# Transformer block and a conditioned norm on one core: row statistics one unit later, and four units of sixteen reduce before they gate

## What is computed

```
def _ada_rmsnorm(x, t, gamma_w, beta_w):
    return (t @ gamma_w.T)[:, None, :] * _rmsnorm(x) + (t @ beta_w.T)[:, None, :]
# attention: 16 heads of 16, softmax(scale * q k^T) v, then W_o
# swiglu: silu(x @ gate_w.T) * (x @ hidden_w.T) @ out_w.T + out_b, 1024 hidden
x = x + a_alpha * _attention(_ada_rmsnorm(x, t, ...), W_q, W_k, W_v, W_o)
x = x + f_alpha * _swiglu(_ada_rmsnorm(x, t, ...), gate_w, hidden_w, out_w, out_b)
# second layer, on the result:
out = (x - mean) * rsqrt(var + EPS) * weight + bias
out = (out + tanh(t @ lin_w.T + lin_b)[:, None, :]) * weight + bias
```

## Time and profile before

| | |
|---|---|
| median of 3 runs | 755.42 us (753.26 to 757.49) |
| profiled execution | 757.3 us, span 755.5 us |
| busy: PE, DVE, ACT, POOL | 94%, 71%, 62%, 52% of the span |
| granted TensorE clock, mean | 0.988 |
| DMA | 107.17 MB, mean 142 GB/s |

### The profile page before, as it was taken

How to read it: one execution, slowest core, us unless ns; L and a number is a source line. 1 busy time by engine, 2 the same in 40 slices (tenths; PEclk the granted TensorE clock), 3 DMA queues, 4 the chain that set the end, 5 groups by cost and what they waited for, 6 DMA issues and landing times.

```text
span 755.5 us, 17410 instructions
## 1 busy us (share of the span) xinstructions
PE 710.5 (94%) x6660; PEld 499.4 (66%) x6660; DVE 533.5 (71%) x797; ACT 466.6 (62%) x860; POOL 391.4 (52%) x493
## 2 busy tenths in 40 slices
PE   5698999999999999999999999999999999999996
PEld 4443435557677667767677677766777667679895
DVE  3877787877577776877677867777677776336765
ACT  4457787776567666775666756675667655753431
POOL 4255142553368534865367543775267444872533
PEclk9879999999999999999999999999999999999998
DMA  8666558355543645263454736255363620332210
GB/s 227 169 211 224 199 175 283 102 183 172 167 135 117 201 148 155 62 217 134 139 163 124 205 107 206 63 179 134 128 178 106 203 81 3 88 96 61 53 48 29
DMA packets 63275, 107.17 MB, mean 142 GB/s; under 512 B 10480, under 2 KB 18344, under 8 KB 63192
## 3 DMA queue, kind: packets, MB, share of 16 engines
q1 hardware_dynamic: 61892, 104.66, 45.1%
q10 hardware_dynamic: 1172, 1.20, 0.6%
q0 software_dynamic: 128, 0.20, 0.1%
HBM read 57.50 MB, written 37.52 MB: 126 GB/s over the span
## 4 chain that ended last, share of the span: by engine, by line
PE 72%; DMA 8%; DVE 8%; ACT 5%; issue 3%; SPq 1%; POOL 1%; ACTq 0%; POOLq 0%; DVEq 0%
PE ps_x L1479 17%; PE ps_o L1455 13%; PE ps_j L1350 11%; PE ps_o L1492 10%; PE ps_s L1439 8%; PE ps_m L1420 6%; DVE mx L1170 3%; ACT prob L963 2%; DMA out_scratch<-o_raw 2%; DMA reciprocal_scratch<-d_s 1%; DMA prob<-in_wk 1%; PE ps_m L1479 1%; PE ps_j L1388 1%; DMA d_c<-reciprocal_scratch 1%; PE ps_s L1479 1%
## 5 line engine op out<-in xcount | busy, mean ns | idle before, releaser
L1170 DVE TENSOR_REDUCE mx<-ps_m 128x2 f32<-128x1024 f32 x211 | 256.9, 1217 | 43.0 <-PE ps_m L1420 42.6
L963 ACT ACTIVATE prob<-ps_s 128x1024 f32<-128x1024 f32 x219 | 223.5, 1020 | 46.6 <-PE ps_s L1439 44.4
L1455 PE MATMUL ps_o<-prob,v 128*32 128x512 f32 x1024 | 128.3, 604 | 0.1
L1439 PE MATMUL ps_s<-qs,ks 64*128 64x512 f32 x438 | 101.2, 456 | 9.6 <-issue 4.4
L670 POOL TENSOR_TENSOR a_lo<-act_y,a_hi 128x256 fp32r<-128x256 f32 x100 | 73.5, 735 | 70.0 <-ACT a_hi L996 70.0
L1211 DVE SCALAR_TENSOR_TENSOR act_y<-act_y,ps_x 128x256 f32<-128x256 f32 x109 | 45.8, 420 | 73.9 <-ACT act_y L989 73.9
L1420 PE MATMUL ps_m<-ks,qs 64*128 64x512 f32 x422 | 90.2, 422 | 8.0 <-DVE mx L1170 4.8
L1479 PE MATMUL ps_x<-n_x,gh_hi 64*128 64x256 f32 x872 | 96.6, 279 | 0.2 <-DMA n_x<-n 0.2
L1479 PE MATMUL ps_x<-n,gh_hi 64*128 64x256 f32 x872 | 96.4, 279 | 0.0
L1439 PEld LDWEIGHTS ps_s<-qs,ks 64*128 64x128 f32 x438 | 41.5, 184 | 77.1 <-issue 52.0
L1479 PEld LDWEIGHTS ps_x<-n,gh_hi 64*128 64x128 f32 x872 | 75.5, 185 | 2.5 <-issue 0.2
(11 more groups left out here) (182 smaller groups left out, 1469.4 us busy)
## 6 DMA issues: line engine op xcount, KB each, us to landing
qs<-stack_scratch SPq DMA_DIRECT2D x30, 512.0 KB, 4.8
ks<-stack_scratch SPq DMA_DIRECT2D x30, 512.0 KB, 6.2
stack_scratch<-qk_hi SPq DMA_DIRECT2D x56, 256.0 KB, 3.4
out_scratch<-o_raw SPq DMA_DIRECT2D x32, 256.0 KB, 2.1
n_x<-n SPq DMA_DIRECT2D x32, 256.0 KB, 3.5
stack_scratch<-qk_lo SPq DMA_DIRECT2D x28, 256.0 KB, 3.9
on_lo<-out_scratch SPq DMA_DIRECT2D x16, 256.0 KB
d_c<-reciprocal_scratch SPq DMA_DIRECT2D x16, 256.0 KB
```

What stands on the lines that cost most here:

```text
L963: act.activation(prob[:, n % 3, 2 * h:2 * h + 2, :], score_pair(n, h)[:], ACT.Exp, scale=SCALE).then_inc(p_r, 1)
L1170: dve.tensor_reduce(mx[:, group % 2, :, h, qt], max_pair(mp)[:], AX.X, ALU.max).then_inc(mx_red, 1)
L1439: mm = pe.matmul(score_pair(n, j)[:, s, :], ks[r:r + 64, g, j, kb * P:(kb + 1) * P], qs[r:r + 64, g, j, :], start=True, stop=True)
L1455: mm = pe.matmul(ps_o[32 * i:32 * i + 32, :], v[:, at:at + 32], prob[:, n % 3, i, :], start=(kb == 0), stop=(kb == TT - 1), skip_group_che ...
```

## The change

Three edits of order; no operation is added or taken away. On the DVE the gate moves behind both reductions in units whose place is 0, 3, 7 or 11 (where the unit has maxima), and `statistics(b - 3, 1)` moves from place 0 to place 1. On SP `store(b - 3, 1)` and `load_tab_b` move behind `max_rows` and what else stands between. On POOL `v_copy(b, 3)` moves ahead of `moments`.

```
+SHORT = (0, 3, 7, 11)
@@ SP, unit(n)
-                if at(2, -3):
-                    store(b - 3, 1)
-                if at(2, -2):
-                    load_tab_b(b - 2)
                 for job in jobs_at(n - 1):
                     if job[:2] == ("FT", 1) and job[2] > 0:
                         swap_halves(job[2], 1)
...
                 if n == UNITS + 2:
                     o_read(0, 1)
                     stack_read(1, 3)
+                if at(2, -3):
+                    store(b - 3, 1)
+                if at(2, -2):
+                    load_tab_b(b - 2)
                 if at(3, -1) and b > 1:
                     rec_write(b - 1, 1)
@@ POOL, unit(n)
+                if at(1, 0) and b > 0:
+                    v_copy(b, 3)
                 if at(1, -3) and b - 3 < B - 1:
                     moments(b - 3, 1)
                     normalise(b - 3, 1)
                     weigh(b - 3, 1)
-                if at(1, 0) and b > 0:
-                    v_copy(b, 3)
@@ DVE, unit(n)
-                    if m == 0 and 0 <= e < TAIL:
+                    if m == (u in SHORT) and 0 <= e < TAIL:
                         gate(e)
...
-                if at(0, -3) and b - 3 < B - 1:
+                if at(1, -3) and b - 3 < B - 1:
                     statistics(b - 3, 1)
```

More of the change, by code:

```diff
@@ L518, in unit @@
                     o_read(b - 1, 1)
[L519 to L522, removed]
                 for job in jobs_at(n - 1):
```

## The result

The changed kernel takes **760.64 us** (median of 5 runs, 757.45 to 761.65) against 755.42 for the kernel before (5 runs in the same group, 753.26 to 757.65): ratio 1.0048, 95% interval 1.0025 to 1.0072; the quotient of the two medians alone would be 1.0069. The forecast was 752.4 and the range 749.2 to 756.5, so it went the other way. Of the 5.2 us between the medians, 3.3 stand between the two profiled executions (757.3 and 760.64; spans 755.5 and 758.8); the other 1.9 is what the profiled execution of before lies above its own median.

A forecast was written before the change was run, and what follows sets the result against it. TensorE was taken as the bound from 200 to 640 us. Gains of 5.8 us less 2.8 in the tail made -3.0: 754.3 us on the profiled scale, 752.4 on the median's, range 749.2 to 756.5.

The forecast's parts named there:

- Gate behind R1: DVE, gate after the unit's second max reduction: TensorE's max matmuls wait less, 2.0 us at places 3 and 11, 0.2 at 7.
- Place 0 and the statistics: Moved statistics free the DVE after place 0: next second max matmul 0.81 us earlier in batches 3 to 6; 3.6 in all.
- beyond it that tanh is late: Unit 67's tanh reads POOL's addition to x and a_lo; 0.8 us of cover, with the tanh late if that is exceeded.
- The store at 352.8 and the table load behind it are out before the reciprocals are ready. Cost in the batches: nothing.: SP's queue in the batches: the later store and table load issue before the reciprocals' write is ready, costing 0 us.
- The tail, +2.8: Late tail statistics delay SP's store, then the reciprocals' write and TensorE's WO job; write taken as 3.4 us, loss 2.8.
- Sum: Whole kernel: gains of 5.8 us less the tail's 2.8 us, so -3.0 us from the profiled execution's 757.3 us.
- C: Rival, chance 0.10: gate ends 0.3 us late, gains vanish, tail loss 2.8 to 3.8 stays; 758.2 to 759.2 us.
- B: Rival, chance 0.13: gate/hidden product waits on the gate, so places 3, 7 and 11 give 0; 754.6 us.
- chance of 0.05 for slower: Probability given to the changed kernel being slower by over 0.5%, that is above 759.2 us.

The follow-up runs named there:

- early_q: tail_back with the write of the next Q ahead of the reciprocals' write on SP from batch 2 on: 749.49 us, ratio 0.9925.
- late_store: tail_back with store of the older half and load of tab_b behind the reciprocals' write on SP in batches 3 to 7: 749.57 us, ratio 0.9925.
- tail_only: Kernel before with only the tail's statistics one unit later (129 and 145 instead of 128 and 144): 761.85 us, ratio 1.0067.
- stats_only: Changed kernel with the gate back where it was before; late statistics and SP's new order stay: 763.69 us, ratio 1.0098.
- tail_back: Changed kernel with the tail's statistics (units 128 and 144) back in their old units: 754.04 us, ratio 0.9977.
- tail_late: Changed kernel, tail statistics still late, with late_store's edit in every batch and in the tail's unit 131: 749.28 us, ratio 0.9916.
- late_all: tail_late with the tail's statistics back in their old units: 747.93 us, ratio 0.9895.
- early_late_all: late_all with early_q's edit as well, Q's write ahead of the reciprocals' write: 749.77 us, ratio 0.9920.
- late_no_short: tail_late with the gate of units 0, 3, 7 and 11 where it was in the kernel before: 755.62 us, ratio 0.9994.
- gate_only: Kernel before with only the gate behind the second maximum in units 0, 3, 7 and 11 of each batch: 753.52 us, ratio 0.9959.
- store_only: Kernel before with only SP's store of the older half and load of tab_b behind the max rows, batches 2 to 7: 755.79 us, ratio 1.0001.

## Why the prediction was wrong

- **Gate behind R1** (forecast 2.0 + 0.2): right in mechanism. After place 3 it gave 0.16 to 0.19 in each of batches 3 to 6, as forecast, and 0.03 in batch 2. After place 11 only 0.28 in all instead of 0.9: S1 there waits for ScalarE's exponential (405.00, S1 at 405.09 in unit 76). After place 7 it gave 0.13 each instead of 0.04. Alone in the kernel before, the edit gives 1.86 us at these places, against the 2.2 forecast.
- **Place 0 and the statistics** (forecast 3.6): right, 3.53. In batch 7 the warning "beyond it that tanh is late" came true: the tanh of unit 115 starts 2.89 after S0 instead of 2.25, behind `a_low`; unit 115 is 0.64 longer, and unit 116 gave back 0.80.
- **"The store at 352.8 and the table load behind it are out before the reciprocals are ready. Cost in the batches: nothing."** This is the step that failed. They are out before, but not landed, and a DMA behind them is done only 0.18 after them. I had the row for it (4.4 right behind the two, against 1.4 alone), used it in the tail, and did not ask what it does in the batches, where the reciprocals' read, the load of xr and Q's write wait on SP behind it. It cost 4.34 us at place 5 in batches 3 to 6, about 1.5 of them by the low clock in unit 69; early_q, late_store and the table show that this chain is the cause. It is also why a faster TensorE turned into a stop: in batch 3 Q's write was issued at 271.28 (before: 271.30), in batch 4 1.1 us earlier, while TensorE's S0 of place 3 came 1.6 and 2.2 us earlier.
- **The tail, +2.8**: the idle is right (2.76), in part by luck: counted from the start of unit 127 the write went 0.4 later than forecast and took 3.02 instead of 3.4. The sum is not right. It had no term for the clock, which stood at 0.50 for 6.8 us around the end of the idle: 2.39 us more. tail_only shows both without the rest of the change.
- **Sum**: forecast -3.0 on the scale of the profiled execution, measured +3.3. Of the 6.3 between, 3.83 are place 5 and 2.4 the clock in the tail.
- **Rivals**: none named this. C was on the right side of zero by a mechanism that did not occur (GH follows M0 by 0.23 to 0.26 after places 0, 3, 7 and 11), and B's did not either. The chance of 0.05 for slower was far too low for a change that moves a DMA on a queue with six transfers behind it; the median of 760.64 lies above the 759.2 that C ended at, the ratio of 1.0048 just inside the 0.5% that the prediction could tell.

## What to carry to other kernels

When an edit moves a DMA on a queue, price every transfer that is issued while it is still in flight (the load took 2.9 us here) with its slow duration, not with the one that it has alone, and follow the chain to the engine that waits last; a queue's order shows issues, but landings decide. An edit that lets the bound engine run ahead makes everything that is tied to another clock relatively late: look at the waits that had little slack before. And a stop of the matmul engine of two to four us may cost twice, once as idle time and once at 1.2 GHz behind it.

## What the runs showed of the hardware

- The 16 KB write of the reciprocals landed 0.16 to 0.18 us behind the 128 KB load issued ahead of it in 11 of the 12 batches 3 to 6 of the changed kernel, stats_only and tail_back.
- From 190 us on the fourteen traces have 116 of these writes at whose issue no other DMA with a known landing was in flight, or none for more than 0.1 us longer. For 74 of them no 16 KB packet of the instruction queue moved meanwhile, and 70 took 1.42 or 1.43 us; the other four (2.27 to 2.61) are those at the start of the tail in tail_late, late_all, early_late_all and late_no_short, behind the load of on_lo. For 42 of them one such packet moved, and all 42 landed 1.03 to 1.18 us behind its end, so that they took 1.41 to 3.41 us. In units 60 and 124 that was so in every trace.
- The granted clock was low for 6.8 us, from 1.1 to 1.8 us before the end of the stop ahead of WO, in all three profiled kernels that stop there for 3.6 to 4.2 us (the changed kernel, stats_only, tail_only) and in none of the others. At shorter stops it fell for 3.4 us in some executions and not in others: behind 1.74 us in unit 69 (changed), 1.55 and 1.80 in unit 37 (gate_only, tail_late), 1.58 in unit 69 (late_all), 1.56 in unit 85 (tail_back), but not behind 1.64 in unit 37 (store_only) and 1.62 to 1.72 in unit 116 (nine traces), while in tail_only and store_only it fell in unit 116 behind 1.02 and 0.54, and in tail_late in unit 30 behind 0.68 and 0.51. What decides between them these runs don't tell.
